# The last feed-forward stage of a decoder kernel: both products alternated per inner block

## The reference

```python
x = _layernorm(x + _L1_attn_ref(x, ...), axis=-1)
x = _layernorm(x + _L1_xattn_ref(x, ctx_1024, ctx_1024, ...), axis=-1)
x = _layernorm(x + _L1_ffn_ref(x, ...), axis=-1)

def _L1_ffn_ref(x, ln_gamma, ln_beta, fc1_q, fc1_scales, fc1_bias, fc2_q, fc2_scales, fc2_bias):
    residual = x
    ...
    h = (x - mu) * jax.lax.rsqrt(var + EPS) * ln_gamma + ln_beta
    y = hf @ w1 + fc1_bias          # 256 -> 1024
    y = jax.nn.silu(y)
    z = y @ w2 + fc2_bias           # 1024 -> 256
    return residual + 0.5 * z.reshape(residual.shape)
```

## Time and the profile before

| what | value |
|---|---|
| median of 3 runs | 1927.8 us |
| lowest and highest run | 1926.09 and 1930.58 us |
| span of the profiled execution | 1928.0 us |
| instructions | 34145 |
| TensorE busy | 1765.4 us (92%) |
| VectorE busy | 1407.8 us (73%) |
| ScalarE busy | 1062.6 us (55%) |
| GpSimd busy | 712.1 us (37%) |
| mean granted TensorE clock | 0.953 |

### The profile page before, as it was taken

One profiled execution on the slowest core, in us unless ns is written; L12 is line 12 of the kernel. 1 busy time (PEld: TensorE's weight loads), 2 busy tenths in 40 slices (PEclk: granted clock), 3 DMA queues, 4 the chain that ended last, 5 costly groups with the idle time before them and its releaser, 6 DMA issues. The chain is left out here.

```text
span 1928.0 us, 34145 instructions
## 1 busy us (share of the span) xinstructions
PE 1765.4 (92%) x13236; PEld 984.1 (51%) x13236; DVE 1407.8 (73%) x2375; ACT 1062.6 (55%) x1722; POOL 712.1 (37%) x789
## 2 busy tenths in 40 slices
PE   8999999989999999789999888599999999999786
PEld 4787577668888888432333454212222222223354
DVE  2524788757777776776777289989999999994563
ACT  1221555535555555235666443178888888886442
POOL 0654977025555554242331134313332121202442
PEclk9999999999999999977999999689999999999898
DMA  5134999776666665441110357411201010100001
GB/s 193 51 102 145 306 316 329 273 267 255 251 252 255 253 250 188 126 137 26 27 35 19 125 159 223 123 45 56 79 19 36 19 33 21 35 2 1 25 12 33
DMA packets 114324, 245.89 MB, mean 128 GB/s; under 512 B 28282, under 2 KB 83102, under 8 KB 110688
## 3 DMA queue, kind: packets, MB, share of 16 engines
q1 hardware_dynamic: 87204, 204.66, 30.8%
q0 software_dynamic: 24848, 36.95, 7.1%
q10 hardware_dynamic: 2112, 2.10, 0.3%
HBM read 180.77 MB, written 62.30 MB: 126 GB/s over the span
## 5 line engine op out<-in xcount | busy, mean ns | idle before, releaser
L2076 DVE TENSOR_REDUCE Eh_maxima<-Eh_max 128x2 f32<-128x802 f32 x512 | 474.7, 987 | 21.6 <-PE Eh_max L1955 16.8
L2064 ACT ACTIVATE Eh_probs<-Eh_pair 128x1024 f32<-128x1024 f32 (+1 forms) x288 | 287.5, 998 | 113.3 <-PE Eh_pair L1994 113.3
L1436 PE MATMUL C_y<-C_x_high,C_W 128*128 128x256 f16 x1472 | 251.0, 274 | 1.5 <-DVE C_x_low L1676 1.5
L1955 PE MATMUL Eh_max<-Eh_KS,Eh_QS 49*128 49x401 f16 x1024 | 197.5, 357 | 45.9 <-DVE Eh_maxima L2076 42.0
L2017 PE MATMUL Eh_av_ps<-Eh_probs,E_V 128*17 128x512 f32 (+1 forms) x1664 | 223.7, 610 | 0.0
L1436 PE MATMUL C_y<-C_x_low,C_W 128*128 128x256 f16 x736 | 201.8, 274 | 0.0
L2076 DVE TENSOR_REDUCE Dh_maxima<-Dh_max 128x2 f32<-128x1024 f32 x128 | 152.1, 1221 | 49.2 <-PE Dh_max L1963 47.3
L2064 ACT ACTIVATE Eh_probs<-Eh_single 128x512 f32<-128x512 f32 x272 | 161.7, 594 | 28.7 <-PE Eh_single L1994 28.7
L1955 PEld LDWEIGHTS Eh_max<-Eh_KS,Eh_QS 49*128 49x128 f16 x1024 | 50.3, 94 | 234.3 <-DVE Eh_maxima L2076 201.3
L1793 POOL DMA_DIRECT2D Eh_KS<-E_kd x64 | 37.1, 579 | 351.0 <-PE Eh_pair L1994 346.2
L1436 PEld LDWEIGHTS C_y<-C_x_high,C_W 128*128 128x128 f16 x1472 | 144.8, 98 | 19.0 <-issue 1.7
(11 more groups left out here) (422 smaller groups left out, 3633.9 us busy)
## 6 DMA issues: line engine op xcount, KB each, us to landing
C_W<-w_split SPq DMA_DIRECT2D x23, 3072.0 KB, 11.5
w_split<-B_w_parts SPq DMA_DIRECT2D x24, 768.0 KB, 9.2
Eh_KS<-E_kd POOLq DMA_DIRECT2D x64, 150.1 KB, 3.3
C_tail<-in_expert_tail_dram SPq DMA_DIRECT2D x23, 384.0 KB, 8.4
B_places<-in_w_experts_dram SPq DMA_DIRECT2D x10, 768.0 KB, 6.6
A_QT<-in_w_experts_dram SPq DMA_DIRECT2D x8, 768.0 KB, 5.1
w_split<-A_QT SPq DMA_DIRECT2D x8, 768.0 KB, 6.6
early_more<-in_w_experts_dram SPq DMA_DIRECT2D x8, 768.0 KB, 11.5
```

The lines of the kernel that those rows point to most:

```text
L1436: last = mm(y_ps[n % Y_BANKS][:, i, :], W[:, u, a, at_w:at_w + P], x[:, s % 2, k, :], start=(q == 0), stop=(q == len(parts) - 1))
L1955: last = self.nc.tensor.matmul(bank[:, a, 0:self.cw], self.QS[r, slot, p, qt * P:(qt + 1) * P], self.KS[r, slot, p, k0:k0 + self.cw], star ...
L2064: self.nc.scalar.activation(dst, src, ACT.Exp, scale=1.0 / SCORE).then_inc(self.exp_done, 1)
L2076: self.nc.vector.tensor_reduce(self.maxima[:, g % 2, :, p * TPB + qt, c], self.max_ps[n % 2][:, :, 0:self.cw], AX_X, ALU.max).then_inc(sel ...
```

## The change

In `phase_last` the second product no longer works by token tile but by inner block. `narrow(n)` takes block n of all four tiles of its chunk into four open accumulators (one bank for each tile), two blocks behind `widen`. Since a block's parts are used up soon, they live in a ring of eight blocks, and ScalarE's cast waits for the block eight before to have been used. The two banks of the output projection are now the two banks of the transposes. The orders on VectorE, ScalarE and GpSimd are laid out anew around it. The biases are loaded by SP at the start of the heads. ScalarE runs one small sigmoid at the heads' end. `normed_again(dve, 1)` moves from the end of the heads to behind `step(0)`. The last chunk's statistics go tile by tile, and its last tile has its own deviation, normalization and store.

```diff
@@ LastStart
-        self.gamma, self.beta = sb("gamma", [P, KD]), sb("beta", [P, KD])
+        self.gamma, self.beta, self.warm = sb("gamma", [P, KD]), sb("beta", [P, KD]), sb("warm", [P, KD])
+        self.b1, self.b2 = sb("b1", [P, NF]), sb("b2", [P, D])
...
         sp.dma_start(self.beta[:], self.dram["L1_ffn_ln_beta"]).then_inc(self.scale_loaded, 16)
+        sp.dma_start(self.b1[:], self.dram["L1_ffn_fc1_bias"]).then_inc(self.small_loaded, 16)
+        sp.dma_start(self.b2[:], self.dram["L1_ffn_fc2_bias"].partition_broadcast(P)).then_inc(self.small_loaded, 16)
+
+    def warm_up(self, act):
+        act.wait_ge(self.scale_loaded, 32)
+        self.nc.scalar.activation(self.warm[:], self.gamma[:], ACT.Sigmoid).then_inc(self.warmed, 1)
...
                 v.tensor_copy(self.HT_parts[:, 0, 0], self.HT[:, 0]).then_inc(self.ht_high, 1)
-                self.normed_again(dve, 1)
@@ phase_cross1, ScalarE
                 heads.scalar(act)
+                start.warm_up(act)
@@ before phase_last
+RING = 8
+STORES = [(c * TPB, (c + 1) * TPB) for c in range(B - 1)] + [(NT - TPB, NT - 1), (NT - 1, NT)]
@@ phase_last
-    hidden, hidden_parts = sb("hidden", [P, 4, S]), sb("hidden_parts", [P, 2, 2, NF, S], F16)
+    hidden, hidden_parts = sb("hidden", [P, 4, S]), sb("hidden_parts", [P, 2, RING, S], F16)
-    after.make_banks(ctx)
-    turn_ps = after.turn_ps
+    turn_ps = after.turn_ps = [ps(f"turn{h}", [P, S])[:] for h in range(KD)]
+    after.out_ps = [bank.rearrange("p (q d) -> p q d", d=D) for bank in turn_ps]
-    y2_ps = [ps(f"y2_{i}", [P, D]) for i in range(2)]
+    y2_ps = [ps(f"y2_{t}", [P, S]) for t in range(TPB)]
@@ SP
-            sp.dma_start(b1[:], dram["L1_ffn_fc1_bias"]).then_inc(small_loaded, 16)
-            sp.dma_start(b2[:], dram["L1_ffn_fc2_bias"].partition_broadcast(P)).then_inc(small_loaded, 16)
             sp.dma_start(w2_parts[:].rearrange("p a k d -> p a (k d)"), weight_parts).then_inc(w_loaded, 16)
-            for c in range(B):
-                sp.wait_ge(norm_out.normed, (c + 1) * TPB)
...
+            for first, end in STORES:
+                sp.wait_ge(norm_out.normed, end)
+                sp.dma_start(out[first * P:end * P, :].rearrange("(t p) d -> p t d", p=P), X[:, first:end, :]).then_inc(stored, 16)
@@ TensorE
-            def narrow(c, t, js):
...
+            def narrow(n):
+                c, j = divmod(n, NF)
+                pe.wait_ge(hidden_low, n + 1)
+                for t in range(TPB):
+                    if j == 0 and c >= 1:
+                        pe.wait_ge(sum_ready, (c - 1) * TPB + t + 1)
                     for i, (a, x) in enumerate(((0, 0), (0, 1), (1, 0))):
+                        last = mm(y2_ps[t][:, 0:D], hidden_parts[:, a, n % RING, t * P:(t + 1) * P], w2_parts[:, x, j, :],
                                   start=(j == 0 and i == 0), stop=(j == NF - 1 and i == 2))
+                    if j == NF - 1 and t < TPB - 1:
+                        last.then_inc(y2_ready, 1)
+                last.then_inc(narrowed, 1)
+            widen(0, 0)
             after.attended(pe, B - 1)
+            widen(0, 1)
             pe.wait_ge(w_loaded, 16)
...
+            for n in range(2, B * NF):
+                widen(*divmod(n, NF))
+                if n == 2:
+                    pe.wait_ge(after.copied, KD * B)
+                    turn(1)
+                if n == 5:
+                    pe.wait_ge(copied, 2 * KD)
+                    after.project(pe, B - 1)
+                if n == NF + 2:
+                    pe.wait_ge(after.sum_ready, NT // 2)
+                    turn(2)
+                if n == 2 * NF + 2:
+                    turn(3)
+                if n < B * NF - 1:
+                    narrow(n - 2)
+            for n in range(B * NF - 3, B * NF):
+                narrow(n)
@@ ScalarE
+                if n >= RING:
+                    act.wait_ge(narrowed, n - RING + 1)
...
+                if n == 0:
                     copy_turned(nc, act, XT, turn_ps, B - 1, after.turned, after.copied)
+                if n == 2:
+                    turn(1)
+                if n == NF + 2:
                     turn(2)
+                if n == 2 * NF + 2:
                     turn(3)
@@ GpSimd
+            for n in range(B * NF):
                 low(n)
+                if n == 2:
+                    start.low(pool, 1)
+                if n == 4:
+                    norm_in.inverse_deviation(pool, 2)
+                if n == NF:
                     after.norm.inverse_deviation(pool, 3)
+                if n == NF + 3:
+                    start.low(pool, 2)
                 if n == NF + 4:
                     norm_in.inverse_deviation(pool, 3)
+                if n == 2 * NF + 3:
+                    start.low(pool, 3)
+                if n in (NF + 5, 2 * NF + 5, 3 * NF + 5):
+                    norm_out.inverse_deviation(pool, n // NF - 1)
+            norm_out.inverse_deviation(pool, B - 1, tiles=(NT - TPB, NT - 1))
+            norm_out.inverse_deviation(pool, B, tiles=(NT - 1, NT))
@@ VectorE
             step(0)
-            start.again(dve, 2)
+            start.normed_again(dve, 1)
             step(1)
+            after.norm.normalize(dve, 2)
             step(2)
+            norm_in.statistics(dve, 2, after.norm.normed)
+            step(3)
             dve.wait_ge(half_b2, 1)
             base(0)
+            for n in range(4, B * NF):
+                c, j = divmod(n, NF)
+                step(n)
+                if n == 5:
+                    start.normed_again(dve, 2)
+                if n == 6:
+                    after.add(dve, 3)
+                    after.norm.statistics(dve, 3, after.sum_ready, per=2)
+                if n == NF:
+                    base(1)
+                if c >= 1 and j == 1:
+                    dve.wait_ge(base_ready, c)
+                    for t in range(TPB):
+                        add((c - 1) * TPB + t)
+                if n == NF + 2:
+                    start.again(dve, 3)
+                if c >= 1 and j == 3:
+                    norm_out.statistics(dve, c - 1, sum_ready)
+                if n == NF + 5:
+                    start.normed_again(dve, 3)
+                if n == NF + 6:
+                    base(2)
+                if n == 2 * NF:
+                    base(3)
+                if c >= 1 and j == 6:
+                    dve.wait_ge(norm_out.rstd_ready, c)
+                    normalize((c - 1) * TPB, c * TPB)
+            dve.wait_ge(base_ready, B)
+            for n in range(NT - TPB, NT):
+                add(n)
+                norm_out.statistics_of(dve, n, sum_ready)
+            dve.wait_ge(norm_out.rstd_ready, B)
+            normalize(NT - TPB, NT - 1)
+            dve.wait_ge(norm_out.rstd_ready, B + 1)
+            normalize(NT - 1, NT)
```

More of the change, by code:

```diff
@@ L3042, in widen @@
                 last.then_inc(y1_ready, 1)
-            def narrow(c, t, js):
-                n = c * TPB + t
-                if js[0] == 0 and n >= 2:
-                    pe.wait_ge(sum_ready, n - 1)
-                if t == 0:
-                    pe.wait_ge(hidden_low, c * NF + js[-1] + 1)
-                for j in js:
+            def narrow(n):
[4 more added lines that the diff above has]
+                        pe.wait_ge(sum_ready, (c - 1) * TPB + t + 1)
@@ L3057, in _ @@
-            turn(1)
-            for j in range(NF // 2):
-                widen(0, j)
-            pe.wait_ge(copied, 2 * KD)
+                    if j == NF - 1 and t < TPB - 1:
+                        last.then_inc(y2_ready, 1)
+                last.then_inc(narrowed, 1)
+            widen(0, 0)
             after.attended(pe, B - 1)
-            for j in range(NF // 2, NF):
-                widen(0, j)
+            widen(0, 1)
             pe.wait_ge(w_loaded, 16)
-            for c in range(1, B):
-                for j in range(NF):
-                    widen(c, j)
-                    narrow(c - 1, j // 2, range(NF // 2) if j % 2 == 0 else range(NF // 2, NF))
-                    if (c, j) == (1, 1):
-                        after.project(pe, B - 1)
-                    if (c, j) == (1, 5):
-                        turn(2)
-                    if (c, j) == (2, 5):
-                        turn(3)
@@ L3075, in _ @@
-            for t in range(TPB):
-                narrow(B - 1, t, range(NF))
+            for n in range(2, B * NF):
[13 more added lines that the diff above has]
+                    narrow(n - 2)
@@ L3096, in high @@
             def high(n):
-                c, j = divmod(n, NF)
                 act.wait_ge(hidden_ready, n + 1)
-                if j == 0 and c >= 2:
-                    act.wait_ge(y2_ready, (c - 1) * TPB)
-                nc.scalar.copy(hidden_parts[:, c % 2, 0, j, :], hidden[:, n % 4, :]).then_inc(hidden_high, 1)
+                if n >= RING:
+                    act.wait_ge(narrowed, n - RING + 1)
+                nc.scalar.copy(hidden_parts[:, 0, n % RING, :], hidden[:, n % 4, :]).then_inc(hidden_high, 1)
```

(18 more changed lines are left out.)

60 lines of the change are left out of this document (5 added, 55 removed).

## The result

The median of the changed kernel is 1910.9 us over six runs (1904.0 to 1914.8), beside 1926.9 for the kernel before on the same chip (six runs, 1920.7 to 1930.6). The ratio is 0.9913, 95% interval 0.9889 to 0.9936: a gain of 0.9%, with medians 16.0 us apart, where 15.9 were forecast. The profiled execution spans 1912.8 us at a mean clock of 0.957 (1928.0 and 0.953 before).

What follows compares the result with a forecast made beforehand. It took TensorE's gaps and matmuls at 1.2 GHz to cost the last stage its time. Heads' end -1.8, TensorE -13.8, tail +0.5, last store -0.8 sum to -15.9: 1928.0 to 1912 us, range 1907 to 1919.5.

Steps and rivals of the forecast that it cites:

- The likeliest case: Whole kernel: everything as forecast, 1912 us, within 1908.5 to 1916; chance 0.53.
- TensorE's term: Last stage: TensorE's work, slow clock and waits take 102.5 us against 116.5, -14.0, counted as -13.8.
- the tail: After TensorE's end: normalization 5.3 us behind instead of 4.8, +0.5; smaller last store, -0.8; what follows landing stays 5.1.
- Heads' end: Before the stage: without the second chunk's renormalization, ScalarE's copy starts about 1794.3 and the table load is hidden; -1.8 us.
- Start: Stage's first blocks: no bias wait, a new wait for second weights, slow clock costing 2.9 us, second product starting at 9.1.
- my fast alternative: Stage's start with TensorE's clock fast in the first matmuls, which would give 1.3 us back.
- the first rival: Fewer waits or a fast start: 1.3 us from the clock, 4 if half the 9.4 is hidden; 1907 us, chance 0.12.
- P: Period of one steady inner block in the last stage: 3P = P + 4.0 + 1.3, so 2.67 us; work alone 2.60.
- Gaps: TensorE's waits in the stage for GpSimd's lows and VectorE's inserts: 9.4 us together, the longest 1.8.
- four falls: Rival: clock falls at the weight wait and three later gaps, costing 6 to 7 us; 1918 us, chance 0.08.
- The doubled low: Rival: every GpSimd low takes about 2.1 us, not 1.16, so period 3.1 to 3.15; 1927 to 1929 us, chance 0.05.
- The hand-laid order is too tight: Rival: hops cost 0.4 us more in sum, the period grows 0.2, 6 us over 30 blocks; 1918 us, chance 0.22.

Runs made afterwards that it cites:

- heads_back: Changed kernel with the second chunk's renormalization back at the end of the heads: 1917.2 us (one run), stage 123.9 us.
- whole_change: The changed kernel run once more unedited, as a yardstick: median 1915.4 us, ratio 0.9924 to the kernel before, stage 121.0 us.
- combined: Changed kernel, second product three blocks behind, weight wait just before first use, output normalizations and base(3) later: median 1910.4 us, ratio 0.9881 to kernel before, stage 111.3.
- low_twice: Changed kernel with GpSimd making each block's low half twice, output unchanged: 1933.2 us (one run), stage 141.6 us.
- turns_only: Kernel before with only the transposed chunks 2 and 3 made three blocks earlier: median 1923.9 us, ratio 0.9994, stage 132.8 us.
- start_turns: Kernel before with early biases, the small sigmoid and the transposed chunks three blocks earlier: median 1916.0 us, ratio 0.9944, stage 127.9 us.
- start_only: Kernel before with only the biases loaded during the heads and the small sigmoid at their end: median 1920.9 us, ratio 0.9976, stage 128.1 us.
- last_whole: Changed kernel with the last chunk's statistics, deviation, normalization and store for all four tiles together: 1915.5 us (one run), stage 120.2 us.
- order: Changed kernel with base(2), base(3) and the output normalizations moved on VectorE: median 1908.1 us, ratio 0.9910 to the kernel before, stage 117.2 us.
- three_behind: Changed kernel with the second product three blocks behind the first instead of two: median 1906.3 us, ratio 0.9910 to the kernel before, stage 117.1 us.

## Why the prediction was right

The forecast was 1912 us, -15.9. It came to 1910.9, -16.0 by the medians and -16.4 by the stage's time. The likeliest case held, by nearly its own sum; but that the sum is met to half a us is luck, for TensorE's term came out 1.5 better and the tail 1.2 worse than forecast:

| term | forecast | measured |
|---|---|---|
| heads' end | -1.8 | 7.01 to 5.17 us from cast to stage: -1.8 |
| stage's first instruction to TensorE's | none | 0.19 to 0.04: -0.15 |
| TensorE in the stage | 116.5 to 102.5, counted -13.8 | 116.4 to 101.1: -15.3 |
| normalization behind TensorE | +0.5 | 4.84 to 4.84: 0 |
| from there to the end | -0.8 | 8.04 to 8.96: +0.9 |
| sum | -15.9 | -16.4 |

*Heads' end: right, with its mechanism.* "The copy starts at about 1794.3": it started at 1795.36, and the cast of this execution came 1.15 later than before's, so 1794.2 in before's time. It waits for the products, as said. The table load fits, by 0.01 us at its end. No drain shows ahead of it (0.01 us), as in the trace before; the 1.4 us that the rule of the Trainium skill (ScalarE: Activation LUTs, What ACT_TABLE_LOAD costs) would have added did not come. heads_back confirms the term by itself.

*Start: the wait is there, the clock was not slow.* I took slow-clock matmuls for the first 5.8 us (2.9 us). In the profiled execution there were none, and N(0) came 7.0 us behind the start, 0.8 sooner than the 7.8 of my fast alternative. It was the "fast start" of the first rival in its first part. The start changes from one execution to the next: of the ten profiles that begin with W(0), three have a fast one. But the slow start was sized too large as well. In whole_change, with a first W of 2.72, N(0) came at 7.9, not 9.1; that slow start cost 0.9. W(2) waited 1.22 for the weights, which landed in 4.8 us, inside my 4.4 to 6.8.

*Steady block: right.* P was 2.65, where 2.67 was worked out, with N waiting for the low by hundredths. Since these are too short to end a group, they sit in "busy": combined does the same 624 matmuls at full clock in 90.9 us, the kernel after in 93.1. So the work is 90.9 (90.2 in my sum), and TensorE stands 8.1 + 2.2 = 10.3 us in all, where I had 9.4. Of the 10.3, 1.2 are the wait for the weights, which my sum with a slow start had at nothing; the rest is 9.1. Then 99.6 + 0.7 + 0.9 = 101.2 with no slow clock: the term came out 1.3 to 1.4 better than its 102.5 because the clock's 2.9 did not arise, less those 1.6. low_twice shows the formula at another value of the low.

*Gaps: the places right, the sizes partly.* Forecast and measured: N(12) 0.65 and 0.39; the seam of the chunks one and two 3.35 in four pieces, the largest 1.8, and 2.50 in four, the largest 1.33; the third turn 0.85 and 0.62; around W(25) 0.65 and none; N(30) 1.45 and 1.12; N(31) 1.35 and 2.17. The last is the one that I sized too small. Multiply(31) could have run from 1892.1, when its sigmoid ends (1891.39 + 0.69); it started at 1894.85, since VectorE first stood 2.36 us for chunk 2's deviation and then normalized for 2.24, as the rows of VectorE above show. No gap ended with slow matmuls, so "four falls" did not happen; the largest was 2.17. My reading behind it, that 2.4 us leave the clock fast and 3.3 do not, is not borne out as a rule: behind a gap of 2.41 the last 96 matmuls started at a granted clock of 1.00 in the kernel before and of 0.53 and 0.50 in turns_only and start_turns, in start_only a W behind 3.29 us was fast (1.47), and in low_twice an N behind 2.31 was slow (2.74). So the count of no falls was right in this case, but not for the reason given.

*Tail: the path was wrong.* The step that failed is the path by which I took the program to end: last normalization, last store, landing, and then "what follows the landing (5.1 us) stays". By the rows the end hangs on GpSimd's last power, 9.46 us ahead of the span's end in every profile, and in the kernel after SP has been done with the last store for 6 us by then. GpSimd's last power ends 3.4 us behind TensorE before and 4.3 after: that is the +0.9 of the table, and it leaves no part for the store. So the forecast's -0.8 for a smaller store bought nothing, though the store did land in 2.5 instead of 2.9, and what follows the landing grew by 1.2. The normalization ends as late behind TensorE as before, not 0.5 later: it ends 6.3 us behind the start of N(31), where I had 6.6, since GpSimd's two deviations take 1.1 and 0.8 us, not 1.3 each, and N(31) itself lasts 1.48, not 1.3. So the last tile's own deviation, normalization and store (a sum of -0.3 in the forecast, from +0.5 and -0.8) are a loss of 0.85, and last_whole shows it. Why GpSimd's DRAIN takes 9.2 us behind its last power is not shown.

*The rivals.* The doubled low is real as a mechanism (low_twice: 141.6, longer than before) but doesn't arise from the change: the lows of the last chunk took 1.15 to 1.16. "The hand-laid order is too tight" was wrong by its number (P didn't grow) but right in that it can be loosened: order and three_behind each take 2.9 to 3.0 off in spite of slow starts, combined 8.8. What my forecast passed over is that this order still left nearly 10 us of the stage to be had. The rule on the shared ports (Trainium skill, SBUF — State Buffer, two separate sides) is borne out where the two engines meet: HT's low took 3.11 us beside a base, 2.13 alone (this happened once in the kernel after too, with base(0)), and four normalizations that met an HT low took 4.21 us, where they take 1.38 alone at the end.

What stays open: the gain of the later weight wait by itself (its kernel had a slow start; in combined it is mixed with the rest), what decides the clock at the stage's start, how much the alternation alone is worth, and why GpSimd's DRAIN at the end takes as long as it does.

## What to carry to other kernels

Where several engines hand a block round in a ring, write the period as an equation of the hops, as 3P = P + 4.0 + 1.3: it tells how far each product may lag. With one block more it is 4P = P + 5.3, so P = 1.8, below the 2.6 of the work, and indeed no N waited for a low until the last; the stage got 3 us shorter (three_behind). Place the inserts of a busy engine by what is queued behind them, and at the end above all, where no later block makes a delay good. Before a last tile is stored alone, find out what the program's end waits for. Here it was not the store but GpSimd's DRAIN, so the smaller transfer bought nothing and the second deviation cost 0.85 us. The list of waits named TensorE's queue; the ends of the engines' own DRAINs told more.

## What the hardware showed that I had not expected

- The part of the program ahead of the stage differs from one execution to the next by up to 13 us (the cast starts at 1786.9 to 1800.1 in the fourteen profiles), while the stage of the unchanged kernel after came out within 1 us twice. So I take most of the spread of the runs to lie there, not in the stage.
- The same first six matmuls of the stage, behind the same pause of 1.15 us, took 1.46 us in three of ten profiles (the kernel after, combined, low_twice) and 2.07 to 2.72 in the other seven. The last 96 matmuls, behind the same gap of 2.41 us, took 10.64 us in two kernels and 12.3 in two others. A single profile can't tell a change of 1 to 2 us at such a place.
- The program ended 9.46 us behind the end of GpSimd's last power in all fourteen profiles, to within 0.01 us; for 9.2 of it GpSimd is in its DRAIN, which ended at least 4.6 us behind SP's.
- GpSimd's power of a tile of four, three and one columns took 1.01, 0.85 and 0.56 us: by an estimate from these it has a fixed part of about 0.4 us (0.56 less a third of the 0.45 between one and four).
- ScalarE's table load took 1.28 us and started 0.01 us behind the activation ahead of it.
